# Moving the outer products and sums of a state-space kernel from a routing stage to the expert stage behind it

## The reference, cut to what matters

```
x = x + 0.5 * L0_ffn(layernorm(x))       # softmax gate over 64 experts, top 8, shared SwiGLU, experts' SwiGLU
x = x + L0_attn(layernorm(x)); x = x + 0.5 * L0_ffn(layernorm(x)); x = x + 0.5 * L1_ffn(...)
x = x + L1_attn(layernorm(x))            # the state-space layer
```

## Time and profile before

| | us |
|---|---|
| three runs, median (lowest, highest) | 3261.39 (3259.48, 3265.24) |
| the profiled execution, time | 3265.29 |
| its span on the profile | 3263.6 |
| busy: PE, PE weight load | 2520.3 (77%), 1645.9 (50%) |
| busy: DVE, ACT, POOL | 2037.2 (62%), 1371.2 (42%), 1781.1 (55%) |

### The profile page before, as it was taken

How to read it: one execution, slowest core, us unless ns; L and a number is a source line. 1 busy time by engine, 2 the same in 40 slices (tenths; PEclk the granted TensorE clock), 3 DMA queues, 4 the chain that set the end, 5 groups by cost and what they waited for, 6 DMA issues and landing times. The chain is left out here.

```text
span 3263.6 us, 68714 instructions
## 1 busy us (share of the span) xinstructions
PE 2520.3 (77%) x24615; PEld 1645.9 (50%) x24634; DVE 2037.2 (62%) x5868; ACT 1371.2 (42%) x2937; POOL 1781.1 (55%) x2004
## 2 busy tenths in 40 slices
PE   3459965778994748999988999592798986999682
PEld 2238863546883434655555555381333333555371
DVE  6873325873334545578855788324999998788513
ACT  2212212321221414266652666343776762566433
POOL 4717762572775303299952133574888885123564
PEclk8679996979997878999987999696899998999796
DMA  9208982222896436011000111222222120111133
GB/s 372 93 10 215 223 191 55 80 79 66 224 231 159 138 79 261 15 19 18 17 3 18 20 29 29 68 80 68 104 79 77 58 99 14 20 24 35 46 96 96
DMA packets 220033, 294.09 MB, mean 90 GB/s; under 512 B 34016, under 2 KB 176895, under 8 KB 213600
## 3 DMA queue, kind: packets, MB, share of 16 engines
q1 hardware_dynamic: 173280, 249.85, 24.7%
q0 software_dynamic: 44352, 39.40, 6.4%
q10 hardware_dynamic: 2112, 1.05, 0.1%
HBM read 181.88 MB, written 100.40 MB: 86 GB/s over the span
## 5 line engine op out<-in xcount | busy, mean ns | idle before, releaser
L3827 POOL TENSOR_TENSOR l3am_db<-l3am_du,l3am_bs 128x1024 f32<-128x1024 f32 x127 | 297.8, 2366 | 38.8 <-DVE l3am_hh L4065 35.1
L4065 DVE TENSOR_TENSOR_SCAN l3am_hh<-l3am_dA,l3am_db 128x1024 f32<-128x1024 f32 x128 | 291.7, 2280 | 0.9 <-ACT l3am_dA L3965 0.7
L1217 POOL TENSOR_TENSOR l2a_pT<-l2a_pT,kept 128x512 int32<-128x512 int32 x213 | 265.0, 1282 | 45.5 <-ACT l2a_pT L1423 45.5
L4196 PE MATMUL l3am_y<-l3am_hc,ident 128*128 128x512 f32 x512 | 242.6, 597 | 9.6 <-DVE l3am_hc L4073 8.7
L3110 POOL DMA_INDIRECT l0f_table<-l0f1e_y,l0f1e_idx x128 | 179.5, 1402 | 116.2 <-DVE l0f1e_idx L3082 67.8
L3110 POOL DMA_INDIRECT l0f_table<-l0f2e_y,l0f2e_idx x128 | 178.8, 1397 | 100.1 <-DVE l0f2e_idx L3082 52.2
L3965 ACT ACTIVATE l3am_dA<-l3am_dl,l3am_al 128x512 f32<-128x512 f32 x256 | 166.3, 682 | 130.8 <-DVE l3am_hh L4065 127.2
L1304 DVE CUSTOM_DVE_ANT_0 l2a_junk<-l2a_s,addend 128x256 f32<-128x256 f32 x486 | 178.1, 421 | 57.0 <-PE l2a_s L1540 44.6
L1297 DVE TENSOR_REDUCE l3f1a_mx<-l3f1a_s 128x2 f32<-128x512 f32 x243 | 156.3, 684 | 40.7 <-PE l3f1a_s L1540 31.9
L1297 DVE TENSOR_REDUCE l3f2a_mx<-l3f2a_s 128x2 f32<-128x512 f32 x243 | 156.2, 684 | 36.1 <-PE l3f2a_s L1540 31.0
L1563 PE MATMUL l2a_e<-l2a_qk 32*128 32x256 f32 x964 | 161.1, 410 | 9.6 <-DVE l2a_pT L1225 8.8
(11 more groups left out here) (854 smaller groups left out, 6892.5 us busy)
## 6 DMA issues: line engine op xcount, KB each, us to landing
l3am_bs<-l3a_b SPq DMA_DIRECT2D x32, 1024.0 KB, 6.5
l0f1m_w<-in_L_ffn_expert_w SPq DMA_DIRECT2D x64, 384.0 KB
l0f2m_w<-in_L_ffn_expert_w SPq DMA_DIRECT2D x64, 384.0 KB
l1a_top<-l1a_kernel SPq DMA_DIRECT2D x16, 1024.0 KB, 12.5
l0f_rows<-blank SPq DMA_DIRECT2D x8, 1930.0 KB, 22.6
l0f1m_w<-in_L_ffn_expert_w SPq DMA_DIRECT2D x64, 192.0 KB
l0f2m_w<-in_L_ffn_expert_w SPq DMA_DIRECT2D x64, 192.0 KB
l3f_rows<-blank SPq DMA_DIRECT2D x8, 1440.0 KB, 11.3
```

The costliest lines, as they stand in the source:

```text
L1217: self.nc.gpsimd.tensor_tensor(t, t, self.kept[:, f // 8 % 2, :].unsqueeze(1).to_broadcast([P, 2, 2 * P]), ALU.mult).then_inc(self.cut_g, 1)
L3827: G.tensor_tensor(db[n % DB][:, :].rearrange("p (j t) -> p j t", j=CC), du[k % 2][:, :, :], bs[s // QUARTER][:, s % QUARTER, :].unsqueeze( ...
L4065: V.tensor_tensor_scan(hh[n % HH][:, :], dA[n % 2][:, :], db[n % DB][:, :], 0.0, ALU.mult, ALU.add).then_inc(h_ready, 1)
L4196: T.matmul(yb[j][:, :], c.ident[:, :], hc[n % 2][:, halves[j]], start=(s == 0), stop=(s == N - 1)).then_inc(summed, 1)
```

## The change

Twelve pieces in each of groups 5 to 7 and the three behind them become 6 pieces in group 5, none in groups 6 and 7, and 2 behind the last addition; the 24 outer pieces, the 7 sums and the last step become a generator of their own, `products`, that DVE steps through in the first expert stage, one piece behind each y(n), so behind units 0 to 30, and the last step behind unit 31. For that, DVE's stream of this expert stage is written out for its 64 units instead of a loop of four. The tiles that both stages need (sn, cs, pr, pi, kk and a copy of D_skip) are allocated around both; the large tiles big and big2 move to the expert stage. SP's store of the kernel moves from the end of its routing stream to the end of its expert stream.

```diff
-        self.big, self.big2 = ph.sb("big", [P, N, 256]), ph.sb("big2", [P, 4, 256])
+    def summing(self, ph):
+        self.big, self.big2 = ph.sb("big", [P, self.N, 256]), ph.sb("big2", [P, 4, 256])
+        self.summed, self.kernel_ready, self.stored = (ph.sem(f"kz_{s}") for s in ("summed", "kernel_ready", "stored"))
...
     def sp_store(self, sp):
-        sp.wait_ge(self.to_act, 4)
+        sp.wait_ge(self.kernel_ready, 1)
         sp.dma_start(self.kz, self.kk[:, :]).then_inc(self.stored, 16)
         sp.wait_ge(self.stored, 16)
...
         link(V.tensor_scalar(di[:, :], ai[:, :], dt[:, 0:1], None, ALU.mult))
+        link(V.tensor_copy(self.dskip[:, :], self.dsk[:, :]))
...
+    def products(self, v):
+        V, N, sn, cs, pr, pi = self.nc.vector, self.N, self.sn, self.cs, self.pr, self.pi
+        big, big2, kk = self.big, self.big2, self.kk
+        done = [0]
+        def link(ins):
+            done[0] += 1
+            ins.then_inc(self.summed, 1)
+            v.wait_ge(self.summed, done[0])
...
         tt(kk[:, 127:W_KZ], big[:, 0, :], big[:, 1, :], ALU.add)
         link(V.tensor_scalar(kk[:, 127:W_KZ], kk[:, 127:W_KZ], 2.0, None, ALU.mult))
-        V.tensor_tensor(kk[:, 127:128], kk[:, 127:128], self.dsk[:, :], ALU.add).then_inc(self.to_act, 1)
+        V.tensor_tensor(kk[:, 127:128], kk[:, 127:128], self.dskip[:, :], ALU.add).then_inc(self.kernel_ready, 1)
...
             for n in range(GROUPS):
                 r.sp_over(sp, n)
-            sk.sp_store(sp)
...
-            PIECES = [(0, 0, 0)] * 3 + [(1, 1, 2), (1, 2, 2)] + [(4, 4, 4)] * 3
+            PIECES = [(0, 0, 0)] * 3 + [(1, 1, 2), (1, 2, 2), (2, 2, 2)] + [(0, 0, 0)] * 2
...
                 for u in range(U):
                     load(i, u)
+            if kernel:
+                kernel.sp_store(sp)
...
-            stream(v, units, V, step)
+            if kernel:
+                products = kernel.products(v)
+                for n in range(units):
+                    step(lambda d: (0, n + d, n + d) if n + d < units else None)
+                    next(products, None)
+                for _ in products:
+                    pass
+            else:
+                stream(v, units, V, step)
```

More of the change, by code:

```diff
@@ L1659, with __init__ @@
 W_KZ = 383
+class KernelParts:
+    def __init__(self, ph):
+        N, M = StateKernel.N, StateKernel.M
+        self.sn, self.cs = (ph.sb(n, [P, N, M]) for n in ("sn", "cs"))
+        self.pr, self.pi = (ph.sb(n, [P, N, 16]) for n in ("pr", "pi"))
+        self.kk, self.dskip = ph.sb("kk", [P, W_KZ]), ph.sb("dskip", [P, 1])
 class StateKernel:
@@ L1672, with __init__ @@
     MAGIC = 1.5 * 2.0 ** 23
-    def __init__(self, ph, w, kz):
+    def __init__(self, ph, w, kz, keep=None):
         self.nc, self.w, self.kz = ph.nc, w, kz
+        keep = keep or KernelParts(ph)
         N, M = self.N, self.M
@@ L1681, in __init__ @@
         self.dr, self.di = ph.sb("dr", [P, N]), ph.sb("di", [P, N])
-        self.argr, self.argi, self.turns, self.mag, self.sn, self.cs = (
-            ph.sb(n, [P, N, M]) for n in ("argr", "argi", "turns", "mag", "sn", "cs"))
+        self.argr, self.argi, self.turns, self.mag = (
+            ph.sb(n, [P, N, M]) for n in ("argr", "argi", "turns", "mag"))
+        self.sn, self.cs, self.pr, self.pi, self.kk, self.dskip = keep.sn, keep.cs, keep.pr, keep.pi, keep.kk, keep.dskip
         self.nr, self.ni, self.tr, self.ti, self.den, self.t0, self.cr, self.ci = (
             ph.sb(n, [P, N]) for n in ("nr", "ni", "tr", "ti", "den", "t0", "cr", "ci"))
-        self.pr, self.pi, self.pt = (ph.sb(n, [P, N, 16]) for n in ("pr", "pi", "pt"))
-        self.big, self.big2 = ph.sb("big", [P, N, 256]), ph.sb("big2", [P, 4, 256])
-        self.kk = ph.sb("kk", [P, W_KZ])
-        self.loaded, self.placed, self.step, self.to_act, self.from_act, self.stored = (
-            ph.sem(f"kz_{s}") for s in ("loaded", "placed", "step", "to_act", "from_act", "stored"))
+        self.pt = ph.sb("pt", [P, N, 16])
+        self.loaded, self.placed, self.step, self.to_act, self.from_act = (
+            ph.sem(f"kz_{s}") for s in ("loaded", "placed", "step", "to_act", "from_act"))
+    def summing(self, ph):
+        self.big, self.big2 = ph.sb("big", [P, self.N, 256]), ph.sb("big2", [P, 4, 256])
+        self.summed, self.kernel_ready, self.stored = (ph.sem(f"kz_{s}") for s in ("summed", "kernel_ready", "stored"))
     def sp_load(self, sp):
@@ L1726, in steps @@
         ar, ai, dr, di, dt, pr, pi, pt = self.ar, self.ai, self.dr, self.di, self.dt, self.pr, self.pi, self.pt
-        big, big2, kk, mf = self.big, self.big2, self.kk, self.mf
+        kk, mf = self.kk, self.mf
         done = [0]
@@ L1810, in steps, with tt @@
         yield
+    def products(self, v):
[6 more added lines that the diff above has]
+            v.wait_ge(self.summed, done[0])
+        def tt(o, a, b, op):
+            link(V.tensor_tensor(o, a, b, op))
         def outer(o, p_, q_, n):
@@ L2810, in clear, with routing_alone @@
                      c.nil[0:SUB, 0:4 * D]).then_inc(m.tables_cleared, 16)
-def routing_alone(nc, c, name, w, m, mats, kernel):
+def routing_alone(nc, c, name, w, m, mats, kernel, parts):
     with Phase(nc, name) as ph:
@@ L2821, in routing_alone @@
         c.kz_of[kernel] = nc.dram_tensor(f"{kernel}_kernel", (D, W_KZ), F32, kind="Internal").ap()
-        sk = StateKernel(ph, w, c.kz_of[kernel])
+        sk = StateKernel(ph, w, c.kz_of[kernel], parts)
         late, c.x_late = c.x_late, False
@@ L2910, in _ @@
             r.pe_out(pe, GROUPS - 1)
+    return sk
 class Matrices:
@@ L2932, with experts @@
     LOADED = 32
-def experts(nc, c, name, w, m, mats, E, C1, KC, A, gated, sub=SUB, U=4, unroll=None):
+def experts(nc, c, name, w, m, mats, E, C1, KC, A, gated, sub=SUB, U=4, unroll=None, kernel=None):
     rows, tables, apart = m.rows, m.tables, m.apart
@@ L2962, in experts @@
             ph.sem(s) for s in ("turned", "xe_ready", "h_done", "s_ready", "g_ready", "o_done", "y_ready", "idx_ready"))
+        if kernel:
+            kernel.summing(ph)
         block = ph.block(drained=False)
@@ L3276, in moe64 @@
         mats = Matrices(outer, w["L0_ffn_expert_w1"], w["L0_ffn_expert_w2"], 6, 3, 4)
-        routing_alone(nc, c, name + "r", w, m, mats, "l1a")
-        experts(nc, c, name + "e", w, m, mats, 64, 6, 3, 2, True)
+        kernel = routing_alone(nc, c, name + "r", w, m, mats, "l1a", KernelParts(outer))
+        experts(nc, c, name + "e", w, m, mats, 64, 6, 3, 2, True, kernel=kernel)
     combine(nc, c, name + "c", m.tables)
@@ L3460, in state_kernel_alone @@
     sk = StateKernel(ph, w, c.kz_of[name])
+    sk.summing(ph)
     block = ph.block()
@@ L3480, in _ @@
         for _ in sk.steps(v):
+            pass
+        for _ in sk.products(v):
             pass
```

## The result

The kernel after takes **3242.32 us** (median of 4 runs, 3241.19 to 3245.68) against 3261.38 for the kernel before in the same comparison (4 runs, 3259.48 to 3265.24). The ratio is 0.9937, with a 95% interval of 0.9921 to 0.9953: 19.1 us less. (The ratios on record are not quotients of the medians, so the two can differ by up to 0.1 per cent.) Both kernels were also profiled twice, the second time in e9 (before) and e8 (after), so each stage has two readings.

A forecast was written before the change was run, and what follows sets the result against it. DVE was taken to bound routing's second half, with POOL, PE and row loads nearly level in the expert stage; -25.9 in routing, +13.5 in the expert stage and -0.8 behind gave -13.2 us: median 3248, range 3238 to 3259.

The forecast's parts named there:

- Routing: Stage before the expert stage: moving pieces and store out brings the first row load 25.9 us earlier, bounds 22 to 29.
- the tail: Routing, last slots to the last addition's end: 13.6 us in place of 14.5, with 11.6 as lower bound.
- clock allowance: Routing's end, last slots to last addition: up to 2.9 us shorter if PE ran at full clock instead of 0.76.
- The two last pieces: Pieces 16 and 17 behind routing's last addition: four DVE instructions 0.73 us apart, 2.9 us.
- the meeting: Engines' meeting between routing and expert stage: 0.7 us kept of the 3.10, bounds 0.4 and 3.1.
- The chain of the unit: Expert stage, units with pieces: y, piece, gT, output, y in series take 3.99 us a unit; 13.5 us lost in all.
- DVE's written-out stream: Expert stage: writing DVE's loop out as 64 units of code costs 0, from -1 to +2 us.
- hidden: Rival, expert stage: the pieces are covered and cost nothing, 3235 us in all; chance 0.08.
- Row waits: Rival, expert stage: PE's row-tile waits stay on top, 4.48 us a unit, 3263 in all; chance 0.08.
- POOL: Rival, expert stage: pieces contend with POOL's scatters, making POOL the bound at 4.65 us a unit, 3270 in all; chance 0.06.
- The store: SP's store, moved to the expert stage's end: costs 0 beside POOL's last scatters, 2.5 us if those didn't cover it.

The follow-up runs named there:

- e9: The kernel before, unchanged, profiled a second time: 3258.49 us, ratio 0.9996.
- e8: The kernel after, unchanged, measured and profiled again: 3246.81 us, ratio 0.9950 to the kernel before.
- e1: The kernel before with only DVE's stream of the first expert stage written out for 64 units instead of looped: 3260.80 us, ratio 0.9987.
- e10: Repeat of e1, the kernel before with only DVE's first expert stage stream written out, profiled again: 3254.09 us, ratio 0.9991.
- e2: The kernel after without the expert stage's pieces, the state kernel's values not computed: 3229.91 us, ratio 0.9895.
- e3: The kernel after with each piece ahead of y(n), behind the copy of idx, instead of behind y(n): 3234.55 us, ratio 0.9909.
- e4: The kernel after with two pieces behind each y, so in units 0 to 15 alone: 3258.19 us, ratio 0.9987.
- e7: e3 with each 128x1024 tensor-tensor replaced by an equally long reduction with one SBUF input, outer products not computed: 3231.12 us, ratio 0.9913.
- e5: The kernel before with SP's store moved behind the expert stage's row loads and DVE's stream there written out, pieces all in routing: 3250.89 us, ratio 0.9969.
- e6: e3 with routing's pieces 10 to 17 spread four each over groups 5 and 6, none behind the last addition: 3233.85 us, ratio 0.9914.

## Why the prediction was right

The forecast was 3248 with a range of 3238 to 3259, by -25.9 in routing, +13.5 in the expert stage and -0.8 behind it. Against means of two profiles each the change gave -27.15, +11.4 and -0.45 (-0.65 and +0.2).

- **Routing.** Groups 5, 6 and 7 end at 148.78, 173.28 and 191.79 (forecast 148.35, 172.2, 191.3). The step that was mis-sized is the tail: 203.37 - 191.79 = 11.6 against 13.6. That is the lower bound given; the whole clock allowance of 2.9 came, at a granted clock of 1.00. The two last pieces took the 2.9 they were given, and the meeting 0.91 in place of 0.7. Row load at 207.14 against 208.5. The gain is steady: from the opening of group 3 to the first row load the kernel before and its variants e1, e9 and e10 take 159.6 to 159.8 us, the kernel after and e2, e3, e4, e7 and e8 131.5 to 132.3. Groups 0 to 2 vary by 2.2 us (group 3 opens at 72.75 to 74.94), but happened to agree within 0.5 in the four profiles of the table.
- **The chain of the unit.** Forecast 3.99 us, measured 3.90 as (342.96 - 218.00) / 32, y(32) being at 342.96. The links are 0.35, 1.24, 0.71 and 1.58 against 0.34, 1.25, 0.71 and 1.69. The last is the mis-sized one, 0.11 * 32 = 3.5 us. The prediction put DVE's written-out stream at 0 (-1 to +2), because straight-line code had shown no gaps; but the 1.69 was read in the looped stream, and written out the step takes 1.58 (e1, e10), whether or not PE waits for gT. e2 confirms the mechanism by taking the pieces away, e3 by moving them to the other side of y, e4 by doubling them. The rival "hidden" holds for e3's place on the path PE and DVE, and not for this one.
- **What it is compared with.** The price of the pieces against the same kernel without them is 13.4 us (e2), against the kernel before 11.4: the kernel before is about 2 us slower in this half (114.60 and 113.01 against 111.54). How much of that is its looped stream and how much variation stays open (e1 and e10, written out, take 113.25 and 110.88).
- **Row waits.** None on top, as argued: with 3.9 us a unit the tiles are there. That rival is out.
- **POOL.** Dismissed on the earlier trace rows, where the row scatters beside pieces were 0.05 us longer. The mean was right, but it was no measure of what a scatter can lose. Of the 23 scatters that begin in 148 to 180, 13 overlap a piece. Eleven of these keep 0.98 us, because they begin ahead of the piece, with it (within 0.02 us), or in its last 0.10 us; two, at 149.24 and 174.28, begin with 0.70 and 0.54 of a piece left and last 1.55 and 1.40. The same holding was there to be read, scatter by scatter.

  In the kernel after it is cheap because of phase. A piece starts as y ends, and 32 scatters begin with 0.15 to 0.33 us of it left: 17 of 128 are above 1.45 us, mostly 1.51, in all 2.6 us. And POOL's 3.4 us a unit has 0.5 to spare under the chain's 3.9: its last scatter of a unit ends 4.5 us behind y in units 8 to 32 alike. In e3 neither holds. So the forecast of no cost came out, but from a mean that depended on where the scatters happened to fall: that part is luck.

  The Trainium skill's page SBUF — State Buffer, section "Who interferes with whom", has the rule that a DVE instruction with two SBUF inputs contends with a GpSimd instruction that reads SBUF, and infers that descriptor writing is left alone by it. e3 against e7 bears out the first (2.05 against 1.40, both begun under the DVE instruction). The scatter's indices lie in SBUF, and no run separates the reading of them from the descriptor writing. So the inference itself is neither shown nor refuted; what the runs show is that such a DVE instruction does hold up an indirect DMA on POOL.
- **The store.** SP issues it at 438.24 with POOL's scatters going on for 18 us more: no cost, as forecast. What its absence took out of the 3.10 us between the stages reached y(0) here, as the time from the first row load to y(0) stayed what it was (10.87 against 11.00); e5, where it became 13.44, shows that this isn't given.
- **Why the median moved by 19 and not by 13.** Routing's 1.3 and the expert stage's 2 more make the mean stage end 16.2 earlier, which is also the size of e8's ratio (16). The other 3 us of the first comparison are of the size by which the same kernel's profiles differ.

## What to carry to other kernels

Work put on an engine with idle time costs its length, less what slack there was, when it stands between the arrival of an input and the instruction that releases the next engine (13.4 us for 31 pieces of 1.25, and the full length for a second piece in e4); the same work one place further on, in the wait for that engine's answer, costs next to nothing on that path (13.4 us against 0.9 up to y(32)), though by the stage's end e3 is 4.7 us above e2, for the most part by the scatters. Before laying DVE work beside a GpSimd indirect DMA, look at the single scatters that begin while such an instruction runs and not at the mean of the group; where the work can be a reduction with one SBUF input, it holds up none. A link's time read in a looped stream is not that of the same link written out (1.69 against 1.58), so compare like with like. Where a shorter end of one stage brings less than its length, look at the granted clock of the next stage's first matmuls (e5, e6).

## What the runs showed of the hardware

- A DVE tensor-tensor with both inputs in SBUF (f32, 1.21 us) holds up a GpSimd indirect scatter that begins while it runs, by what is left of it less 0.13 us: a scatter-add of 80 rows took up to 2.25 us in place of 1.40 in e3, a row scatter 1.55 in place of 0.98 in the kernel before. 28 of 30 that began ahead of it were not held, two were, by its whole length (2.75 and 2.77). A reduction of the same length with one input doesn't hold a scatter (1.40), nor does a tensor-tensor with one input in PSUM (gT, 1.40); a tensor-scalar of 128x1024 in 0.69 us does (1.15 in place of 0.98). The pieces that hold a scatter up keep their own 1.21 us.
- In DVE's looped stream y starts 0.11 us later behind output's first load than in the written-out one (1.69 and 1.58; units 4 to 59 of the kernel before, and no unit of e1 or e10).
- The time from the first row load to y(0), with the same instructions, is 10.9 to 11.0 us at a granted clock of 0.68 or 0.69 (before, after, e3), and 13.0 and 13.4 at 0.61 and 0.53 (e6, e5). Before e5's and e6's low clock the engines' meeting was short (0.7 us in e5); but after's was too (0.9), so what sets it is not settled.
- Over 84 us with PE busy for 71% (e4) the granted clock was 0.90, in spells of 1.2 GHz between longer ones of 2.4 GHz; over 20 us of another stage, also 71% busy, it was 1.00. These rows don't show why.
